# A graph diffusion followed by a selected LSTM: zeros, degree, reciprocal, low parts and the first block's weight rows are done in another way

## The reference

```
xn     = y * rsqrt(sum(y*y))                         # y = layernorm(x)
sup_e  = edge_weight_e * exp(<xn[row], xn[col]> / (4 e^(2 sigma)))   # 1 where row == col
norm   = segment_sum(sup, row)                       # the degree
denom  = b + norm * a + a
repeat 10: out = (y * b + (segment_sum(sup * out[col], row) + out) * a) / denom
x = x + out
z = layernorm(x)
for t in rows:                                       # one after the other
    s = argmax([h, c, z_t] @ W_sel.T + b_sel)
    g = z_t @ W_ih[s].T + h @ W_hh[s].T + b_ih[s] + b_hh[s]
    i, f, g, o = g;  c = sigmoid(f)*c + sigmoid(i)*tanh(g);  h = sigmoid(o)*tanh(c)
x = x + h
```

## Time and profile before

| | |
|---|---|
| median of three runs | 6861.82 us |
| the profiled execution | 6865.91 us |
| its span in the profile | 6864.2 us |
| TensorE busy | 6126.8 us (89%) |
| VectorE busy | 3617.9 us (53%) |
| ScalarE, GpSimd busy | 1804.5 us (26%), 1685.8 us (25%) |
| mean granted clock of TensorE | 0.955 of full |
| moved by DMA | 389.97 MB |

### The profile page before, as it was taken

How to read it: one execution, slowest core, us unless ns; L and a number is a source line. 1 busy time by engine, 2 the same in 40 slices (tenths; PEclk the granted TensorE clock), 3 DMA queues, 4 the chain that set the end, 5 groups by cost and what they waited for, 6 DMA issues and landing times.

```text
span 6864.2 us, 340774 instructions
## 1 busy us (share of the span) xinstructions
PE 6126.8 (89%) x126674; PEld 4106.7 (60%) x126675; DVE 3617.9 (53%) x19152; ACT 1804.5 (26%) x6561; POOL 1685.8 (25%) x4128
## 2 busy tenths in 40 slices
PE   6727999679999999999999999999999999999986
PEld 3423444566666666666666666666666666666664
DVE  5453111235555556555665555566556665565555
ACT  1001000412233233222332332233333333233321
POOL 5732111412222222222222222222222222222220
PEclk8758999579999999999999999999999999999999
DMA  3220000522222122222222222222222222222210
GB/s 94 1 77 0 0 0 0 177 70 60 60 61 61 57 61 62 58 60 61 64 63 61 62 61 61 60 62 64 61 61 63 64 63 61 60 63 61 61 52 27
DMA packets 715589, 389.97 MB, mean 57 GB/s; under 512 B 47835, under 2 KB 703579, under 8 KB 715296
## 3 DMA queue, kind: packets, MB, share of 16 engines
q1 hardware_dynamic: 684322, 369.66, 18.4%
q0 software_dynamic: 24192, 0.10, 1.1%
q10 hardware_dynamic: 7038, 19.69, 0.9%
HBM read 370.96 MB, written 18.38 MB: 57 GB/s over the span
## 4 chain that ended last, share of the span: by engine, by line
PE 70%; issue 6%; DVE 6%; DMA 0%; DVEq 0%; SPq 0%; POOL 0%; ACT 0%; POOLq 0%
PE ps L1007 33%; PE ps L1069 15%; PE ps L1016 8%; PE ps L1000 5%; PE ps L996 4%; DVE hsum L837 2%; PE ps L993 2%; PE ps L983 2%; DVE osum L845 1%; DVE acts L855 1%; DVE gates L842 1%; DVE osum L848 1%; DVE cprod L851 0%; PE ps L972 0%; DMA wring<-in_w_ih 0%
## 5 line engine op out<-in xcount | busy, mean ns | idle before, releaser
L1007 PE MATMUL ps<-WH,hparts 128*2 128x384 f16 x49760 | 2297.3, 326 | 194.4 <-issue 173.2
L837 DVE TRANSPOSE_TENSOR_REDUCE hsum<-ps 128x12 f32<-128x384 f32 x1250 | 728.8, 583 | 1784.5 <-PE ps L1007 1774.2
L1007 PEld LDWEIGHTS ps<-WH,hparts 128*2 128x2 f16 x49760 | 1042.4, 83 | 1046.7 <-issue 297.0
L1069 PE MATMUL ps<-xcur,wcur 128*128 128x64 f32 x9728 | 1342.8, 281 | 89.1 <-issue 15.1
L1069 PEld LDWEIGHTS ps<-xcur,wcur 128*128 128x128 f32 x9728 | 1179.3, 191 | 276.6 <-issue 213.6
L449 POOL COPY xT<-hfull 128x4 f32 x1250 | 239.5, 192 | 3721.7 <-DVE hfull L866 3721.7
L465 POOL COPY wcur<-wring 128x512 f32<-128x512 f32 x1216 | 743.4, 611 | 449.7 <-ACT gxb L593 447.8
L1016 PEld LDWEIGHTS ps<-WH,hparts 128*2 128x2 f16 x40000 | 596.7, 83 | 359.0 <-issue 316.6
L1016 PE MATMUL ps<-WH,hparts 128*2 128x128 f16 x40000 | 775.4, 219 | 8.6
L578 ACT ACTIVATE gx_now<-gxb 128x16 f32 x1250 | 269.7, 216 | 1832.6 <-DVE pick L831 1709.3
L963 PE MATMUL ps<-O,Adj 128*128 128x512 f16 x3000 | 650.3, 380 | 77.2 <-DVEq L743 77.2
(11 more groups left out here) (147 smaller groups left out, 5001.8 us busy)
## 6 DMA issues: line engine op xcount, KB each, us to landing
wring<-in_w_ih SPq DMA_DIRECT2D x1280, 256.0 KB, 2.9
gxb<-in_w_hh ACTq DMA_DIRECT2D x32, 512.0 KB, 4.0
adjacency<-Adj SPq DMA_DIRECT2D x2, 6400.5 KB, 24.7
Adj<-adjacency SPq DMA_DIRECT2D x10, 640.0 KB, 7.3
sim<-adjacency SPq DMA_DIRECT2D x10, 640.0 KB, 6.5
adjacency<-total,where_ POOLq DMA_INDIRECT x168
x_rows<-X SPq DMA_DIRECT2D x1, 2560.0 KB, 8.7
wring<-x_rows SPq DMA_DIRECT2D x10, 256.0 KB, 3.6
```

Source lines behind the costliest of these rows:

```text
L837: dve.tensor_reduce(hsum[:, :], gate_ps.rearrange("p (c q) -> p c q", q=32), AX.X, ALU.add, apply_transpose=True).then_inc(turned, 1)
L1007: last = nc.tensor.matmul(gate_ps[32 * j:32 * j + 2, :], hparts[:, k, :], WH[:, s * KC + k, part, j, 0:3 * P], start=(k == 0 and part == 0 ...
L1069: last = nc.tensor.matmul(unit_ps, wcur[:, k, :], xcur[:, k, :], start=(k == 0), stop=(k == KC - 1))
```

## The change

Five parts:

- Only 3201 of the 12801 columns of `Adj1` are cleared, and after the tiles of the edges instead of before them. The zeros go to HBM in eight DMAs of a quarter of the columns each, all from the same columns.
- The degree product runs by block of rows: three matmuls for block `r` as soon as `adj_ready` has reached `r + 1`, into three PSUM banks that accumulate side by side.
- The diagonal blocks are picked from PSUM first, and the sums and the reciprocal are taken of 128 x 10 values. TensorE spreads the result: ten matmuls of ones with diagonal matrices (`adiag`, in the tiles `kdiag`, `same`, `junk`), and three copies bring it from PSUM to `inv_b`.
- The low part of M goes from GpSimd to VectorE, one block behind.
- The first block's projection has the k-pieces on the outside: slot `k` of the ring holds the k-piece of four units, which is one row of 2 KB per partition in HBM where it was four of 512 bytes. A group of four units is 16 matmuls with one wait for `proj_mm` at its end.

```diff
--- before.py
+++ after.py
@@ -45,6 +45,8 @@
     NN = NP * NP
     CW = NN // P + 1
     ITERS = 10
+    ZC = -(-CW // 4)
+    ZEROS = [(z, min(ZC, CW - z)) for z in range(0, CW, ZC)]
     COLS = [(c, min(512, NP - c)) for c in range(0, NP, 512)]
     TB = 64
     BLOCKS = -(-N // TB)
@@ -135,6 +137,7 @@
         XB = adj_words[:, 0:RT * D].rearrange("p (t d) -> p t d", t=RT)
         T = adj_words[:, RT * D:2 * RT * D].rearrange("p (t d) -> p t d", t=RT)
         inv_b = sim[:, 0, :]
+        adiag = [one[:, q, :] for one, part in ((kdiag, range(NQ)), (same, range(NQ)), (junk, range(2, NQ))) for q in part]
 
 
         WH = sb("WH", [P, S * KC, 2, 4, D], f16)
@@ -213,6 +216,8 @@
         sim_exp = sem("sim_exp")
         adj_ready = sem("adj_ready")
         deg_mm = sem("deg_mm")
+        adiag_set = sem("adiag_set")
+        arow_mm = sem("arow_mm")
         prop_mm = sem("prop_mm")
         m_ready = sem("m_ready")
         m_high = sem("m_high")
@@ -288,7 +293,8 @@
 
             sp.wait_ge(zero_set, 2)
             for b in range(2):
-                sp.dma_start(adj[b].rearrange("(p n) -> p n", p=P), Adj1[:, :]).then_inc(adj_zeroed, 16)
+                for z0, zn in ZEROS:
+                    sp.dma_start(adj[b].rearrange("(p n) -> p n", p=P)[:, z0:z0 + zn], Adj1[:, 0:zn]).then_inc(adj_zeroed, 16)
 
             for b in range(2):
                 sp.wait_ge(scattered[b], 16 * EIT * (NQ // 2))
@@ -315,9 +321,11 @@
 
             with sp.Fori(0, S) as q:
                 for g in range(G):
-                    for u in range(SUB):
-                        sp.wait_ge(wring_free, sp.snap(q * (G * SUB) + (g * SUB + u + 1)))
-                        load_unit(q, g, u)
+                    for k in range(KC):
+                        sp.wait_ge(wring_free, sp.snap(q * (G * KC) + (g * KC + k + 1)))
+                        sp.dma_start(wring[:, k, :, :].rearrange("p u n -> p (u n)"),
+                                     w_ih[:, bass.ds(q, 1), order[g], k * D:(k + 1) * D].rearrange("p a n -> p (a n)")
+                                     ).then_inc(wring_in[k], 16)
             sp.wait_ge(lx_out, 16)
             sp.dma_start(pick_row[0:1, :], pick_dram.rearrange("(a t) -> a t", a=1)).then_inc(rows_in, 16)
             sp.wait_ge(wring_free, UNITS + SUB)
@@ -358,7 +366,7 @@
 
             last_word = pool.alloc_register("last_word")
             pool.reg_mov(last_word, P * CW - 1)
-            pool.wait_ge(adj_zeroed, 32)
+            pool.wait_ge(adj_zeroed, 16 * 2 * len(ZEROS))
             for q in range(NQ):
                 pool.sem_inc(places_free[q], 1)
 
@@ -402,10 +410,6 @@
                 landed(2, second)
             landed(3, 32 * EIT)
 
-            for r in range(RT):
-                pool.wait_ge(m_high, r + 1)
-                pool.tensor_tensor(M_parts[:, 1, r, :], Adj[:, r, :], M_parts[:, 0, r, :], ALU.subtract).then_inc(m_low, 1)
-
             def low_part(new, r, n):
                 pool.wait_ge(t_high, n)
                 pool.tensor_tensor(new[:, 1, r, :], T[:, r, :], new[:, 0, r, :], ALU.subtract).then_inc(t_low, 1)
@@ -612,12 +616,12 @@
                 dve.wait_ge(v, chain[0])
 
             dve.memset(X[:, RT - 1, :], 0.0).then_inc(zero_set, 1)
-            dve.memset(Adj1[:, :], 0.0).then_inc(zero_set, 1)
             dve.memset(ones[:, :], 1.0).then_inc(consts, 1)
             dve.memset(ident[:, :], 0.0).then_inc(consts, 1)
             dve.memset(src_i[:, :], 0)
             dve.memset(dst_i[:, :], 0)
             dve.memset(ew[:, :], 0.0).then_inc(edge_ready, 1)
+            dve.memset(Adj1[:, 0:ZC], 0.0).then_inc(zero_set, 1)
             for s in range(S):
                 link(dve.memset(ramp[:, s:s + 1], float(S - s)))
 
@@ -718,22 +722,32 @@
                 dve.tensor_tensor(Adj[:, r, :], Adj[:, r, :], Adj1[:, r * NP:(r + 1) * NP], ALU.mult).then_inc(adj_ready, 1)
 
             dve.wait_ge(deg_mm, 1)
+            for r in range(RT):
+                link(dve.scalar_tensor_tensor(out=junk[:, 0, :], in0=ps[:, r // 4, (r % 4) * P:(r % 4 + 1) * P], scalar=1.0, in1=ident[:, :],
+                                              op0=ALU.mult, op1=ALU.mult, accum_out=den[:, r:r + 1]))
+            link(dve.tensor_scalar(den[:, :], den[:, :], ab[:, 0:1], ab[:, 1:2], ALU.mult, ALU.add))
+            link(dve.tensor_scalar(den[:, :], den[:, :], ab[:, 0:1], None, ALU.add))
+            link(dve.reciprocal(den[:, :], den[:, :]))
+            link(dve.tensor_scalar(adn[:, :], den[:, :], ab[:, 0:1], float(2 ** MS), ALU.mult, ALU.mult))
+            for r in range(RT):
+                dve.tensor_scalar(adiag[r], ident[:, :], adn[:, r:r + 1], None, ALU.mult).then_inc(adiag_set, 1)
+            link(dve.tensor_scalar(bdn[:, :], den[:, :], ab[:, 1:2], float(2 ** OS), ALU.mult, ALU.mult))
+            dve.wait_ge(arow_mm, RT)
             for c, (c0, m) in enumerate(COLS):
-                link(dve.tensor_scalar(inv_b[:, c0:c0 + m], ps[:, c, 0:m], ab[:, 0:1], ab[:, 1:2], ALU.mult, ALU.add))
-            link(dve.tensor_scalar(inv_b, inv_b, ab[:, 0:1], None, ALU.add))
-            link(dve.reciprocal(inv_b, inv_b))
-            for r in range(RT):
-                link(dve.scalar_tensor_tensor(out=junk[:, 0, :], in0=inv_b[:, r * P:(r + 1) * P], scalar=1.0, in1=ident[:, :],
-                                              op0=ALU.mult, op1=ALU.mult, accum_out=den[:, r:r + 1]))
-            link(dve.tensor_scalar(adn[:, :], den[:, :], ab[:, 0:1], float(2 ** MS), ALU.mult, ALU.mult))
-            link(dve.tensor_scalar(bdn[:, :], den[:, :], ab[:, 1:2], float(2 ** OS), ALU.mult, ALU.mult))
-            link(dve.tensor_scalar(inv_b, inv_b, ab[:, 0:1], float(2 ** MS), ALU.mult, ALU.mult))
+                link(dve.tensor_copy(inv_b[:, c0:c0 + m], ps[:, 4 + c, 0:m]))
+
+            def low_of_m(r):
+                dve.wait_ge(m_high, r + 1)
+                dve.tensor_tensor(M_parts[:, 1, r, :], Adj[:, r, :], M_parts[:, 0, r, :], ALU.subtract).then_inc(m_low, 1)
 
             for r in range(RT):
                 link(dve.tensor_tensor(Adj[:, r, :], Adj[:, r, :], inv_b, ALU.mult))
                 blk = Adj[:, r, r * P:(r + 1) * P]
                 dve.scalar_tensor_tensor(out=blk, in0=ident[:, :], scalar=adn[:, r:r + 1], in1=blk,
                                          op0=ALU.mult, op1=ALU.add).then_inc(m_ready, 1)
+                if r > 0:
+                    low_of_m(r - 1)
+            low_of_m(RT - 1)
 
             dve.wait_ge(m_low, RT)
             for r in range(RT):
@@ -942,11 +956,15 @@
             for q in range(NQ):
                 pe.wait_ge(edge_out[q], EIT)
 
-            pe.wait_ge(adj_ready, RT)
-            for c, (c0, m) in enumerate(COLS):
-                for r in range(RT):
+            for r in range(RT):
+                pe.wait_ge(adj_ready, r + 1)
+                for c, (c0, m) in enumerate(COLS):
                     last = nc.tensor.matmul(ps[:, c, 0:m], ones[:, :], Adj[:, r, c0:c0 + m], start=(r == 0), stop=(r == RT - 1))
             last.then_inc(deg_mm, 1)
+
+            for r in range(RT):
+                pe.wait_ge(adiag_set, r + 1)
+                nc.tensor.matmul(ps[:, 4 + r // 4, (r % 4) * P:(r % 4 + 1) * P], ones[:, :], adiag[r], start=True, stop=True).then_inc(arow_mm, 1)
 
             pe.wait_ge(prop_ready, 1)
             with pe.Fori(0, ITERS // 2) as i:
@@ -975,15 +993,20 @@
             pe.wait_ge(lx_ready, 1)
 
             with pe.Fori(0, SG) as q:
-                for u in range(SUB):
-                    pe.wait_ge(wring_in[u], pe.snap(q * 16 + 16))
-                    pe.sem_inc(pieces_seen, 1)
-                    pe.wait_ge(proj_out, pe.snap(q * SUB + (u + 1)))
-                    for k in range(KC):
-                        last = nc.tensor.matmul(ps[:, 4 + u, 0:TB], wring[:, u, k, :], xT[:, k, 0:TB], start=(k == 0), stop=(k == KC - 1))
-                    last.then_inc(proj_mm, 1)
-                    pe.wait_ge(proj_mm, pe.snap(q * SUB + (u + 1)))
-                    pe.sem_inc(wring_free, 1)
+                for k in range(KC):
+                    for u in range(SUB):
+                        if u == 0:
+                            pe.wait_ge(wring_in[k], pe.snap(q * 16 + 16))
+                            pe.sem_inc(pieces_seen, 1)
+                        if k == 0:
+                            pe.wait_ge(proj_out, pe.snap(q * SUB + (u + 1)))
+                        last = nc.tensor.matmul(ps[:, 4 + u, 0:TB], wring[:, k, u, :], xT[:, k, 0:TB], start=(k == 0), stop=(k == KC - 1))
+                        if k == KC - 1:
+                            last.then_inc(proj_mm, 1)
+                        elif u == SUB - 1:
+                            last.then_inc(wring_free, 1)
+                pe.wait_ge(proj_mm, pe.snap(q * SUB + SUB))
+                pe.sem_inc(wring_free, 1)
 
             for b in range(WB):
                 pe.wait_ge(whh_low[b], WIT + 1)
```

## The result

The changed kernel takes 6832.65 us in the median of 5 runs (6826.91 to 6835.89), the kernel before 6864.96 beside it: a ratio of 0.9953, 95% interval 0.9939 to 0.9968. That is 32 us less where 75 were forecast. The profiled execution took 6835.89 us with a span of 6833.9.

A forecast was written before the change was run, and what follows sets the result against it. The unedited LSTM, with TensorE as the chain, was taken to bound four fifths of the span. Gains of 10.5 + 20.3 + 3.8 + 10.9 + 29.8 = 75.3 us, less 4.1 for the profiled run, gave 6787 us, range 6762 to 6806.

The forecast's parts named there:

- Start: Clearing of `Adj1` at the kernel's start: a quarter left, hidden behind the edges' loads; gain 10.5 us, bounds 8.5 and 10.7.
- Degree: Degree product by block hides behind the adjacency's blocks, leaving 3.3 us after the last; gain 20.3 us, bounds 15 and 21.3.
- Reciprocal: Between degree product and M: picking diagonals first takes 12.4 us instead of 16.17; gain 3.8 us.
- Low parts: Ten blocks of M: low part on VectorE at 1.48 us, 3.21 a block; gain 10.9 us, other bound -1.
- First block: LSTM input's first block on TensorE: unbroken groups take 8.22 us instead of 10.12, sixteen groups; gain 29.8 us.
- the rival of a rising clock: First block's longer stretches lift TensorE to 2.4 GHz, about 33 us more gain, 6754 us; chance 0.12.
- The late ring: First block: slow landings make seven groups wait 2.2 us each, 15 us, 6802; chance 0.11 together with other weak cases.
- The LSTM's steps, unchanged: LSTM loop: bodies are the same, so steps stay as long as before; wrong if the mean moves over 0.01 us.
- the rival that it isn't: LSTM steps lengthen as programs ahead of the loops change length and branches lie elsewhere; doubled idle gives 6959 us; chance 0.03.

The follow-up runs named there:

- e4: Only the first block's edit (2 KB rows, k loop outermost) on the kernel before: 6833.53 us against 6863.46.
- e5: Kernel before with 21 more VectorE instructions ahead of the loops, putting `hsum` at 428: 4.3677 us a step, 63 us slower than 6864.38.
- e14: Changed kernel with one more instruction heading VectorE's loop body, loop start held, `hsum` at 429: came out at the expected 4.30 us a step, 6762 us.
- e15: Kernel before with 20 more VectorE instructions ahead of the loops and one heading the body, `hsum` at 428: came out at the expected 4.368 us a step, 6928 us.
- e18: Changed kernel with one semaphore for both of `hsum`'s conditions, no separate wait, one more instruction ahead, `hsum` at 428: 4.2794 us a step.
- e1: Changed kernel with one more VectorE instruction (a short memset) ahead of the LSTM's loops: 6762.72 us, 4.3025 us a step.
- e7: Changed kernel with two more VectorE instructions ahead of the loops, `hsum` at 430: 6760.18 us, 4.2963 us a step.

## Why the prediction was wrong

The forecast of 6787 (75.3 us less) was wrong by 46 us, beyond its range. By its own steps, in differences between the two traces:

- *Start, 10.5.* Right: the last block of the adjacency is done 11.1 us earlier (458.50 to 447.36). `x` was awaited until 13.30, half a us past the 12.8 forecast and short of the 14 at which the step would have been wrong. The first scatter is at 51.43 for 50.1. The zeros landed at 44.3 and not by 43: they left from 5.7 on, beside `x`, and took 38.6 us. The scatter's sums covered that, as forecast.
- *Degree, 20.3.* Right, 21.2: the picks begin 32.3 us earlier (482.21 to 449.87), 11.1 of them inherited. 2.5 us stand behind the last block, where 3.3 were taken: its six matmuls took 2.42 at full clock, a little over the 2.2 reckoned for that clock. That the last block met the full clock is part luck: the two blocks ahead of it began at half, behind 2.22 us without work, and took 6.23.
- *Reciprocal, 3.8.* Right in kind, 5.4: 10.76 us from the picks to the first block of M (449.87 to 460.63) where 12.4 had been worked out. The diagonals' matmuls did take 2.08 for the first eight, but 1.64 for the next, and the copies 1.88 for L722's 2.23.
- *Low parts, 10.9.* Right, 11.1: 1.49 on VectorE, as its own row of the same width said, not GpSimd's 2.61; L746 fell back to 0.35.
- *First block, 29.8.* Right, 33.1 (81.9 to the first step, 48.8 of them before): a steady group takes 7.99, not 8.22, since its boundary fell to 0.91 from the 1.15 that was taken over. The clock stayed at 0.50, and e4 confirms the part alone with 29.9. The rule in the page "TensorE: Matmul & The Clock Gate" of the Trainium skill, section "Why this matters for your kernels", to keep TensorE busy so that it leaves the half rate, didn't act on these stretches of 7 us with under 1 us between them: the measurement is against it here, and the rival of a rising clock with it. The late ring didn't come either: once the first slot was in, TensorE waited for the DMA three times (0.47, 0.21 and 1.27 us). The DMA engines stood at 0.83 for 283 GB/s, not at the 0.93 reckoned for 277.
- *The LSTM's steps, unchanged.* This is the step that failed, and the only one. I took the mean step as given because the bodies are the same instructions, and gave 0.03 to the rival that it isn't. The step moved by 0.042 us, four times the 0.01 that the prediction named as a sign of being wrong: (4.3567 - 4.3150) x 1249 is 52 us lost against a gain of 82 that all five terms delivered. The rival was right in that the length of the code ahead of the loops counts. It named VectorE's program among others, but rested on TensorE's idle time and on the branches; what costs is one VectorE instruction behind its separate wait (e5, e14, e15, e18). The row it rested on, TensorE's idle time under "issue" ahead of L1007, pointed to the wrong engine: in the profile after it didn't grow,

```profile
L1030 PE MATMUL ps<-WH,hparts 128*2 128x384 f16 x49760 | 2297.7, 326 | 189.2 <-issue 156.8
L851 DVE TRANSPOSE_TENSOR_REDUCE hsum<-ps 128x12 f32<-128x384 f32 x1250 | 728.5, 583 | 1875.3 <-PE ps L1030 1875.3
```

  and the loss stands in VectorE's idle time, under the name of TensorE's products, 1875.3 us for the 1780.4 of e1 in the same row. Nothing in that row says that the products had been done.

The place's price has two parts, by comparing the changed kernel with e7: right steps 3.8226 for 3.7775 us, some 940 of them, 42 us; wrong ones 5.937 for 5.841, some 304, 29 us. With 4 of the few long steps that is the 75 between 4.3567 and 4.2963 over 1249 steps.

So at an ordinary place the change is worth 101 to 104 us (6863.46 - 6762.72 in e1, 6864.38 - 6760.18 in e7) and not 75. 82 of them lie ahead of the LSTM; the other 20 or so are in it: 4.2963 to 4.3025 a step against 4.3134 to 4.3150 in the kernel before at ordinary places. The traces show three parts. The tenth step took 10.96 us before, and 10.25 in e5, but 5.94 to 6.05 in e4, e1, e7 and the changed kernel: 5 us. A step with a wrong guess takes 5.841 us in e7 for 5.871: 9 us. One with a right guess takes 3.778 for 3.783: 5 us. The rest lies in other long steps. The first two show on TensorE as idle time under "issue": 3.84 us ahead of the unit (L1069) in the tenth step of the kernel before, and 0.57 us in the mean ahead of the repeated products for 0.53 in e7. That the place of TensorE's code is behind them wasn't tried, and stays open; the first block's edit with its 3 instructions less took only the first of them away, and its wrong steps were longer (5.899).

What the hardware does at places 428 and 556 is open too. The runs show where it is and what it costs, not what is fetched there.

## What to carry to other kernels

A body that isn't edited can still change its time when code ahead of it changes length: after any edit, compare the mean step of each untouched loop between the two traces before believing or rejecting the edit, and shift the loop by an instruction or two if it moved. Where a loop's step hangs on the last of several conditions, fold them into one semaphore that is counted by each, so that the waiting instruction holds the only wait; here that was worth 20 us, and the place 428 then cost nothing. And where two conditions must stay apart, the separate wait belongs on the one that comes first in most steps; in the built programs here it got the condition that was written last.

## What the runs showed of the hardware

- On VectorE `hsum` behind a separate wait that passes last starts 0.09 us after it, but 0.20 where it is instruction 428 or 556 of the program; 407 to 409, 412, 427, 429, 430, 436, 460 and 492 are ordinary. It cost 66 us (e5 beside the kernel before) to 75 us (the changed kernel beside e7) in 1249 steps. Whether other instructions behind a wait pay the same was not tried.
- Without a separate wait ahead of it, the same instruction at 428 loses nothing (4.2794 us a step, and 4.2798 at 427).
- Two stretches of f32 matmuls, both less than 1 us apart, got different clocks. Six of the ten blocks of the degree product (128x512) hold 1.00 over 2.42 us each, five of them 0.66 to 0.95 apart. The clock rose from 0.50 to 1.00 within the first two, and behind an idle time of 2.22 us the clock was down again: 0.69 in the mean from 441 to 446. The first block's groups (128x64,'s kind) hold 0.50 over 7.08 us each, from 1234 to 1298 as shown. Why the two differ stays open. Of the degree product in the changed kernel, in order of time, and by stretch:

```profile
426.51 2.42 PE L962 MATMUL ps<-Adj,ones 128*128 128x512 f32 x6 [0.75 <-DVE Adj L722]
429.82 2.42 PE L962 MATMUL ps<-Adj,ones 128*128 128x512 f32 x6 [0.90 <-DVE Adj L722]
```
```profile
433.00:434.00 1.00, 1.00 (x3) 0.52 (x4) 1.00 (x1) 0.00 (x0) 0.00 (x0) 1.00 1.04 411
```
